# The products that find the softmax maxima read fp16 copies of queries and keys, in the first two softmax attentions

## The chip, the cores and the metric

The kernel runs on one core of one Trainium2 chip. The time is device microseconds of that core. Its engines work side by side and meet at semaphores: PE (TensorE; PEld is its weight load), DVE (VectorE), ACT (ScalarE), POOL (GpSimd), and SP, which issues transfers. Matrix products go to PSUM, of which this kernel's attention uses 8 banks.

## The reference

Eight stages work on an `x` of 16 sequences of 128 tokens, 256 channels each, and each stage adds to it: a correlation attention, a quantised feed-forward, a windowed softmax attention, a feed-forward over soft slots, a full softmax attention, a receptance feed-forward, a rotary softmax attention and a routed feed-forward. The change concerns the windowed and the full one. Both compute, with 16 heads of 16 channels,

```python
Q = (query @ Wq.T + bq).reshape(b, s, N_HEADS, HEAD_DIM).transpose(0, 2, 1, 3)
K = (key @ Wk.T + bk).reshape(b, s, N_HEADS, HEAD_DIM).transpose(0, 2, 1, 3)
scores = jnp.einsum('bhqd,bhkd->bhqk', Q, K) * scale
scores = jnp.where(mask[None, None], scores, jnp.float32(-jnp.inf))   # windowed one only
attn = jax.nn.softmax(scores, axis=-1)
out = jnp.einsum('bhqk,bhkd->bhqd', attn, V)
```

where the query is the layer-normalised `x`, and key and value are the context. A softmax is the same whatever value is subtracted from a row's scores, so the maximum that is subtracted need not be exact.

## The kernel before

`attention` runs three times: windowed, full, and rotary. Its work has two parts.

Projections. PE projects keys, values and then queries; a job is one half of the channels (`o`, 2 of them) of four sequences (`g`, 4 groups). ACT writes the keys to `KT` and the queries, in two variants by the parity of the head, to `QT` (two activations a job, L978); both are fp32. The first maxima are made inside: PE's query jobs go g = 0, 1, 2, then `maxima(0)`, then g = 3. In the windowed and the full attention DVE has nothing to do in the query projections until then.

The loop over tiles. A tile is one sequence, n = 0 to 15, with its 16 heads. For each tile the scores are computed twice. `maxima(n)` on PE (L824) makes them with the queries in the rows: for each of HR = 4 slots and R = 4 groups of 32 partitions, a product with 32 x 128 weights (`QT`) and 128 columns (`KT`). DVE reduces them over the keys, in two instructions of two banks each (L1105), to negated maxima in bf16. PE turns these (L831), ACT copies them out (L989). `scores(n)` (L844) makes the scores again, with the keys in the rows, 8 products of 256 columns, and `shift(n)` (L855) adds the negated maxima with 16 products in bf16, again of 32 x 128 weights and 128 columns. ACT takes the exponentials (L995, two instructions), `weigh_values` (L867) multiplies by the values, ACT copies the sums (L1007), PE turns them (L874), DVE divides (L1111, L1114), PE turns the attended rows (L881), ACT copies (L1002), PE multiplies by the output weights (L888), DVE adds to `X` (L1120). In the windowed attention `add_window` (L807) writes the mask to the banks ahead of maxima and scores.

PE's order in an iteration n is written out by hand: turn_maxima(n), maxima(n+1), turn_sums(n-2), output(n-3), scores(n), turn_attended(n-2), shift(n), weigh_values(n-1). DVE's is maxima(n+1) first half, add_bias(n), normalise(n-2), add_output(n-3), maxima(n+1) second half, statistics. ACT's is attended_out(n-2), exponentials(n) first half, sums_out(n-1), maxima_out(n+1), exponentials(n) second half. `hold_clock` (L55) gives PE products that nobody reads, at the ends and in the first two iterations.

The scores go round a ring of 6 banks, 4 for a tile. So `scores(n)` waits for DVE's first half of `maxima(n+1)`, whose banks it takes over, and for the exponentials of the tile before; `maxima(n+1)` waits for the first exponentials of tile n-1; `turn_attended(n-2)` waits for `add_output(n-3)`; `shift(n)` waits for the copied maxima.

## Time and profile before

| | us |
|---|---|
| runs, median of three | 2104.43 (2100.67 to 2106.3) |
| profiled execution, its own time | 2108.12 |
| profiled execution, span from first to last instruction | 2105.8 |
| PE busy | 1866.5 (89%) |
| DVE busy | 1507.5 (72%) |
| ACT busy | 1122.6 (53%) |

The mean granted clock of TensorE over the span was 0.953 of full speed. The profile is one execution. A row of a timeline gives the start from the span's beginning, the time until the end of the last instruction that is merged into the row, and in brackets how long the engine had been idle and what ended that. An fp32 product leaves two records, so 16 of them are "x32"; a 16-bit one leaves one. In "at_ps<-at_KT,at_QT" the tile written stands left; "32*128" is the part of the array in use. The windowed attention lies at about 327 to 483 us of the span, the full one at 1386 to 1525; the rotary one enters its loop near 1670.

### The profile page before, as it was taken

Reading aid. Unit: us, or ns where it says so; the run is one execution under the profiler, and the core shown is the slowest. Engines: PE = TensorE matmul, PEld = TensorE weight load, DVE = VectorE, ACT = ScalarE, POOL = GpSimd, SP = SyncE. Lnnn points to the kernel's source line nnn. Section 1 sums busy time; section 2 is a strip of 40 time slices with the busy share of each in tenths; the row PEclk is TensorE's granted clock in tenths of the full one; section 3 lists DMA queues with packets and bytes.
Section 4 is the critical chain, followed back from the end, with each engine's and each line's share of the span. In section 5 each row is a group of like instructions: output and inputs, shape, how many; then the busy total and the mean of one; then the engine's idle time right before and its main releaser. Section 6 shows DMA issues by size and latency. Waiting matters only on the chain. (4 is left out here: it accounts for less than half of the span.)

```text
span 2105.8 us, 42222 instructions
## 1 busy us (share of the span) xinstructions
PE 1866.5 (89%) x16876; PEld 1371.4 (65%) x16876; DVE 1507.5 (72%) x3163; ACT 1122.6 (53%) x1896; POOL 155.6 (7%) x121
## 2 busy tenths in 40 slices
PE   7969268997799999999999999989896898599995
PEld 6844055765377766666667777656674577598884
DVE  6887875566777777777777776766666666688886
ACT  3536754446256656666666655435441455366772
POOL 0001300000000000000000000000000000144441
PEclk9979689998999999999999999999999999699997
DMA  6120001002100000000000000010001001567775
GB/s 216 46 77 0 0 1 52 2 3 91 41 21 21 21 21 21 24 33 26 21 21 21 1 1 1 1 51 2 2 21 54 1 2 35 172 226 259 258 239 188
DMA packets 80370, 120.98 MB, mean 57 GB/s; under 512 B 9841, under 2 KB 62513, under 8 KB 80049
## 3 DMA queue, kind: packets, MB, share of 16 engines
q1 hardware_dynamic: 75760, 106.22, 15.2%
q0 software_dynamic: 4416, 12.06, 1.6%
q8 instruction: 136, 2.23, 0.4%
q14 instruction: 58, 0.47, 0.1%
HBM read 103.58 MB, written 14.68 MB: 56 GB/s over the span
## 5 line engine op out<-in xcount | busy, mean ns | idle before, releaser
L2523 PE MATMUL sl_ps_eo<-sl_w,sl_hT 128*128 128x256 f16 x3072 | 354.2, 274 | 0.8 <-DVE sl_hT L2766 0.7
L2500 PE MATMUL sl_ps_h<-sl_slot_inT,sl_w 128*128 128x512 f16 x1536 | 339.1, 380 | 0.5 <-ACT sl_h L2643 0.5
L2523 PEld LDWEIGHTS sl_ps_eo<-sl_w,sl_hT 128*128 128x128 f16 x3072 | 299.1, 98 | 36.3 <-DVE sl_hT L2766 1.3
L2643 ACT ACTIVATE sl_h<-sl_ps_h,sl_b1T 128x512 f32<-128x512 f32 x256 | 175.7, 687 | 171.0 <-PE sl_ps_h L2500 163.9
L2500 PEld LDWEIGHTS sl_ps_h<-sl_slot_inT,sl_w 128*128 128x128 f16 x1536 | 150.2, 98 | 176.7 <-ACT sl_h L2643 2.4
L2766 DVE TENSOR_TENSOR sl_hT<-sl_h,sl_hT 128x512 f16<-128x512 f32 x256 | 176.9, 692 | 102.1 <-ACT sl_hT L2646 97.8
L1105 DVE TENSOR_REDUCE at_neg_max<-at_ps 128x8 bf16<-128x1024 f32 x96 | 116.9, 1221 | 127.4 <-PE at_ps L824 127.4
L2062 PE MATMUL mo_ps_h<-mo_xgT,mo_w 128*128 128x256 f16 x1104 | 126.4, 275 | 2.7 <-issue 1.4
L2780 DVE SCALAR_TENSOR_TENSOR sl_result<-sl_ps_eo,sl_b 128x256 f32<-128x256 f32 x128 | 54.3, 424 | 97.6 <-PE sl_ps_eo L2523 93.2
L2073 PE MATMUL mo_ps_eo<-mo_w,mo_hT 128*128 128x256 f16 x1104 | 124.1, 273 | 0.0
L2062 PEld LDWEIGHTS mo_ps_h<-mo_xgT,mo_w 128*128 128x128 f16 x1104 | 108.4, 99 | 17.9 <-issue 4.3
L2073 PEld LDWEIGHTS mo_ps_eo<-mo_w,mo_hT 128*128 128x128 f16 x1104 | 107.1, 98 | 12.0
L995 ACT ACTIVATE at_probT<-at_ps 128x1024 f32<-128x1024 f32 x96 | 98.6, 1027 | 19.4 <-PE at_ps L855 19.4
L2125 ACT ACTIVATE mo_h<-mo_ps_h,mo_b 128x256 f32<-128x256 f32 x184 | 77.4, 478 | 55.3 <-issue 51.1
L1166 POOL MEMSET at_v<- 128x2048 f32 x6 | 10.7, 1817 | 1140.7 <-POOLq L85 1140.7
L1002 ACT ACTIVATE at_attT<-at_ps 128x256 f32<-128x256 f32 x48 | 18.4, 384 | 140.4 <-PE at_ps L881 140.4
L2145 POOL DMA_INDIRECT mo_xg<-x_rows,mo_from_i x46 | 65.5, 1425 | 237.3 <-DVE mo_from_i L2236 222.0
L2646 ACT ACTIVATE sl_hT<-sl_h 128x512 f16<-128x512 f32 x128 | 80.6, 629 | 4.1
L2622 ACT ACTIVATE sl_combT<-sl_ps_lt 128x512 f32<-128x512 f32 x32 | 19.1, 597 | 110.3 <-PE sl_ps_lt L2479 110.3
L1552 PE MATMUL qf_ps<-qf_xqT,qf_w_inT 128*128 128x512 f16 x288 | 67.0, 394 | 8.6 <-DVE qf_xqT L1751 6.2
L2254 DVE SCALAR_TENSOR_TENSOR mo_w<-mo_w_raw,mo_w 128x1024 f16<-128x1024 f32 x46 | 56.0, 1220 | 15.3 <-ACT mo_w L2107 15.3
L2248 DVE TENSOR_TENSOR mo_hT<-mo_h,mo_hT 128x512 f16<-128x512 f32 x92 | 63.8, 693 | 3.2
(429 smaller groups left out, 3674.4 us busy)
## 6 DMA issues: line engine op xcount, KB each, us to landing
mo_w_raw<-in_L_ffn_W SPq DMA_DIRECT2D x46, 1024.0 KB, 7.7
sl_w_in<-in_L_ffn_w SPq DMA_DIRECT2D x16, 1024.0 KB, 5.3
at_ctxT<-ctx_pairs SPq DMA_DIRECT2D x9, 512.0 KB, 7.6
mo_w_raw<-pair_rows SPq DMA_DIRECT2D x4, 1024.0 KB, 8.9
mo_b<-in_L_ffn_b SPq DMA_DIRECT2D x23, 128.0 KB
ac_attention_w<-L_attention_w SPq DMA_DIRECT2D x3, 768.0 KB, 11.6
w_pairs<-ac_w_pair SPq DMA_DIRECT2D x3, 768.0 KB, 3.2
ac_ctx_all<-in_ctx SPq DMA_DIRECT2D x4, 512.0 KB, 8.2
```

What stands on the lines that cost most here:

```text
L995: act.activation(probT[:, n % 2, 2 * pair:2 * pair + 2].rearrange("p r j q -> p r (j q)"), ps[:, at:at + 2], ACT.Exp, scale=SCALE).then_in ...
L1105: dve.tensor_reduce(neg_max[:, 2 * pair:2 * pair + 2, 0:HR], ps[:, at:at + 2].rearrange("p r (j k) -> p r j k", j=HR), AX.X, ALU.max, nega ...
L1552: last = pe.matmul(pair(q)[:, g], w_inT[:, w, i, k, c * P:(c + 1) * P], xqT[:, x, k, tokens], start=(k, a) == (0, 0), stop=(k, a) == (C - ...
L2062: last = pe.matmul(ps_h[:, q % 3, j % 2], w1_of(m, wp)[:, k, j * P:(j + 1) * P], xgT[:, m % 2, xp, k], start=(k, a) == (0, 0), stop=(k, a) ...
L2073: last = pe.matmul(ps_eo[:, s, 0:D], hT[:, m % 2, hp, j, s * P:(s + 1) * P], w2_of(m, wp)[:, j], start=(j, a) == (0, 0), stop=(j, a) == (H ...
L2125: act.activation(h[:, q % 2, j % 2], ps_h[:, q % 3, j % 2], ACT.Relu, bias=b1[:, m % WB, j:j + 1], scale=1.0 / W_SCALE).then_inc(h_ready, 1)
L2145: pool.indirect_dma_start(xg[:, m % XB, s], None, env.x_rows, bass.IndirectOffsetOnAxis(ap=from_i[:, q:q + 1].bitcast(U32), axis=0)).then_ ...
L2500: last = pe.matmul(ps_h[:, j % 2], w1[:, e % 2, w, k, j * P:(j + 1) * P], slot_inT[:, q % 2, x, k].rearrange("p b s -> p (b s)"), start=(k ...
L2523: last = pe.matmul(ps_eo[:, b % 2, 0:D], hT[:, hp, j, b * P:(b + 1) * P], w2[:, e % 2, w, j], start=(j, a) == (0, 0), stop=(j, a) == (HJ - ...
L2643: act.activation(h[:, j % 2], ps_h[:, j % 2], ACT.Gelu, bias=b1T[:, q // G4, j:j + 1], scale=1.0 / W_SCALE).then_inc(h_ready, 1)
L2646: act.activation(hT[:, 0, j], h[:, j % 2], ACT.Copy).then_inc(h_high, 1)
L2766: dve.tensor_tensor(hT[:, 1, j], h[:, j % 2], hT[:, 0, j], ALU.subtract).then_inc(h_split, 1)
```

## The change

In the windowed and the full attention the operands of L824 are fp16 copies. `QT_half` is a new tile; the keys' copy lies in the memory of the context tile, which is no longer read once all values are projected. DVE makes them: four copies of 1024 elements for the keys and eight of 1024 for the queries in each of the two attentions, placed in its queue ahead of, between and behind the first maxima. PE waits for them ahead of every `maxima(n)`. In the rotary attention the names point to the fp32 tiles, and nothing changes. `scores(n)`, which feeds the exponentials, stays fp32.

```diff
--- before.py
+++ after.py
@@ -651,6 +651,11 @@
         ctxT = t.sb("ctxT", [P, G4 - 1, 2, C, 4, L], F16)
         QT = t.sb("QT", [P, C, B, 2, L])
         KT = t.sb("KT", [P, C, B, L])
+        if rotary:
+            QT_max, KT_max = QT, KT
+        else:
+            QT_max = t.sb("QT_half", [P, C, B, 2, L], F16)
+            KT_max = ctxT[:].rearrange("p g a c b l -> p (g a c b l)")[:, 0:C * B * L].rearrange("p (c b l) -> p c b l", c=C, b=B)
         v1 = t.sb("v1", [P, B, HR, R, 32])
         neg_max = t.sb("neg_max", [P, R, 32], BF16)
         neg_maxT = t.sb("neg_maxT", [P, P], BF16)
@@ -675,6 +680,7 @@
         plain_ready, swap_made = t.sem("plain_ready"), t.sem("swap_made")
         v_made, v_ready = t.sem("v_made"), t.sem("v_ready")
         x_turned, x_high, x_split = t.sem("x_turned"), t.sem("x_high"), t.sem("x_split")
+        k_half, q_half = t.sem("k_half"), t.sem("q_half")
         max_made, max_ready = t.sem("max_made"), t.sem("max_ready")
         max_turned, maxT_ready = t.sem("max_turned"), t.sem("maxT_ready")
         shifted, prob_ready = t.sem("shifted"), t.sem("prob_ready")
@@ -814,6 +820,9 @@
                 if n == 0:
                     pe.wait_ge(proj_out, JOBS + C)
                     pe.wait_ge(v_ready, B)
+                if not rotary:
+                    pe.wait_ge(k_half, G4)
+                    pe.wait_ge(q_half, C * (n // 4 + 1))
                 enough(pe, max_ready, 2 * n)
                 enough(pe, prob_ready, 2 * (n - 2) + 1)
                 if windowed:
@@ -821,7 +830,7 @@
                 for j in range(HR):
                     for r in range(R):
                         rows = slice(32 * r, 32 * r + 32)
-                        last = pe.matmul(ps[:, ring_bank(first, r), j * P:(j + 1) * P], QT[rows, j // 2, n, j % 2], KT[rows, j // 2, n],
+                        last = pe.matmul(ps[:, ring_bank(first, r), j * P:(j + 1) * P], QT_max[rows, j // 2, n, j % 2], KT_max[rows, j // 2, n],
                                          start=not windowed, stop=True, skip_group_check=windowed)
                 last.then_inc(max_made, 1)
 
@@ -1098,6 +1107,15 @@
                 dve.wait_ge(x_high, n + 1)
                 dve.tensor_tensor(xT[:, 1, :, n], x_bank(n), xT[:, 0, :, n], ALU.subtract).then_inc(x_split, 1)
 
+            def keys_half(g):
+                dve.wait_ge(v_made, B)
+                dve.wait_ge(proj_out, C * (g + 1))
+                dve.tensor_copy(KT_max[:, :, 4 * g:4 * g + 4], KT[:, :, 4 * g:4 * g + 4]).then_inc(k_half, 1)
+
+            def queries_half(g, o):
+                dve.wait_ge(proj_out, JOBS + C * g + o + 1)
+                dve.tensor_copy(QT_max[:, o, 4 * g:4 * g + 4], QT[:, o, 4 * g:4 * g + 4]).then_inc(q_half, 1)
+
             def maxima(n, pair):
                 dve.wait_ge(max_made, n + 1)
                 enough(dve, max_turned, n)
@@ -1141,6 +1159,12 @@
                 if rotary:
                     for o in range(C):
                         queries_turned(g, o)
+                else:
+                    if g == 0:
+                        for k in range(G4):
+                            keys_half(k)
+                    for o in range(C):
+                        queries_half(g, o)
                 if g == FIRST_MAXIMA:
                     for pair in range(2):
                         maxima(0, pair)
```

## Rows read from the trace of the kernel before

**Rows 1.** The page, part 1: busy us (share of the span) and instructions by engine.
```profile
PE 1866.5 (89%) x16876; PEld 1371.4 (65%) x16876; DVE 1507.5 (72%) x3163; ACT 1122.6 (53%) x1896; POOL 155.6 (7%) x121
```

**Rows 2.** Table by stretches, full attention: us, busy us by engine, granted clock, DMA.
```profile
1420.00:1520.00 100.00, 92.63 (x1704) 68.55 (x1702) 64.56 (x130) 53.10 (x85) 0.00 (x0) 1.00 0.01 3
```

**Rows 3.** Timeline, a tile of the windowed loop: start, us, engine, line, operation, [idle].
```profile
433.12 0.23 PE L831 MATMUL at_ps<-at_ident_b,at_neg_max 128*128 128x128 bf16 x1
...
433.95 1.17 PE L824 MATMUL at_ps<-at_KT,at_QT 32*128 32x128 f32 x32
...
435.06 0.66 PE L874 MATMUL at_ps<-early_ident,at_sumsT 128*128 128x128 f32 x4
435.19 1.22 DVE L1105 TENSOR_REDUCE at_neg_max<-at_ps 128x8 bf16<-128x1024 f32 x1 [2.81 <-PE at_ps L824]
...
436.53 0.39 PEld L807 LDWEIGHTS at_ps<-at_window_b,at_ident_b 64*64 64x64 bf16 x8 [0.36 <-issue]
...
438.56 0.40 PE L855 MATMUL at_ps<-at_neg_maxT,at_slot_sel 32*128 32x128 bf16 x16
...
438.90 1.08 PE L867 MATMUL at_ps<-at_probT,at_v 128*32 128x128 f32 x32
...
439.91 0.23 PE L831 MATMUL at_ps<-at_ident_b,at_neg_max 128*128 128x128 bf16 x1
```

**Rows 4.** Timeline, a tile of the full attention's loop.
```profile
1492.65 0.23 PE L831 MATMUL at_ps<-at_ident_b,at_neg_max 128*128 128x128 bf16 x1
...
1492.93 1.17 PE L824 MATMUL at_ps<-at_KT,at_QT 32*128 32x128 f32 x32
...
1494.16 1.22 DVE L1105 TENSOR_REDUCE at_neg_max<-at_ps 128x8 bf16<-128x1024 f32 x1 [1.87 <-PE at_ps L824]
...
1495.50 0.77 PEld L844 LDWEIGHTS at_ps<-at_QT,at_KT 32*128 32x128 f32 x16 [0.35 <-issue]
...
1496.26 0.41 DVE L1120 TENSOR_TENSOR X<-X,at_ps 128x256 f32<-128x256 f32 x1
...
1496.78 0.20 PEld L881 LDWEIGHTS at_ps<-early_ident,at_att 128*128 128x128 f32 x2 [0.51 <-DVE at_att L1114]
...
1498.50 0.23 PE L831 MATMUL at_ps<-at_ident_b,at_neg_max 128*128 128x128 bf16 x1
```

**Rows 5.** Timeline, the full attention's last tile, with no L824.
```profile
1510.20 0.23 PE L831 MATMUL at_ps<-at_ident_b,at_neg_max 128*128 128x128 bf16 x1
...
1510.99 0.42 PEld L874 LDWEIGHTS at_ps<-early_ident,at_sumsT 128*128 128x128 f32 x4 [0.69 <-ACT at_sumsT L1007]
...
1511.48 1.03 PE L888 MATMUL at_ps<-at_wo,at_attT 128*128 128x256 f32 x4
...
1512.44 1.15 PE L844 MATMUL at_ps<-at_QT,at_KT 32*128 32x256 f32 x16
```

**Rows 6.** Timeline, full attention, from its query projections into the loop.
```profile
1419.96 2.36 DVE L1105 TENSOR_REDUCE at_neg_max<-at_ps 128x8 bf16<-128x1024 f32 x2 [9.20 <-PE at_ps L824]
1421.33 2.79 ACT L978 ACTIVATE at_QT<-at_ps,at_bq_parity,at_parity_scale 128x512 f32<-128x512 f32 x4 [0.77 <-PE at_ps L755]
...
1424.17 0.23 PE L831 MATMUL at_ps<-at_ident_b,at_neg_max 128*128 128x128 bf16 x1 [0.92 <-ACT at_QT L978]
...
1425.57 1.23 DVE L1105 TENSOR_REDUCE at_neg_max<-at_ps 128x8 bf16<-128x1024 f32 x1 [3.26 <-PE at_ps L824]
```

**Rows 7.** Groups by line and form, DVE, whole span: count, busy us, mean ns.
```profile
L2764 DVE CAST sl_hT<-sl_h 128x512 f16<-128x512 f32 x128 | 53.7, 419 | 3.4 <-ACT sl_h L2643 3.4
...
L2825 DVE CAST sl_row_sel<-early_ident 128x2048 bf16<-128x2048 f32 x1 | 1.2, 1219 | 0.0
```

**Rows 8.** Rotary attention: timeline rows after an idle PE, then a stretch of the table.
```profile
1670.15 0.23 PE L831 MATMUL at_ps<-at_ident_b,at_neg_max 128*128 128x128 bf16 x1 [2.19 <-ACT at_QT L975]
...
1670.31 1.64 PE L824 MATMUL at_ps<-at_KT,at_QT 32*128 32x128 f32 x32
...
1672.50:1675.00 2.50, 2.50 (x23) 2.12 (x26) 2.19 (x3) 0.00 (x0) 0.00 (x0) 0.65 0.00 0
```

## The prediction

> **What bounds the kernel now.** I read the page first, then a table by stretches, then the timeline of one tile in each of the two loops that the change reaches. The page gives TensorE 1866.5 us busy of a span of 2105.8 us [rows 1], but that is an average over eight stages, so it only says where to look. The table for the full attention, from the handover out of its projections to the last tile, shows PE busy 92.63 of 100 us at a granted clock of 1.00, the 2.4 GHz level [rows 2]. A busy PE here is not an engine that nobody holds up. So the question is which wait ends last inside a tile.
>
> The windowed attention repeats a tile every 439.91 - 433.12 = 6.79 us [rows 3], the full one every 1498.50 - 1492.65 = 5.85 us [rows 4]. In both, PE turns the maxima (L831), makes the products for the next maxima (L824), turns the sums (L874), makes the output (L888) and the scores (L844), turns the attended rows (L881), shifts (L855) and weighs the values (L867). What leaves L824 is picked up by DVE at L1105, the first reduction of a pair, and PE may not write the scores until that reduction is done, since they go to its banks. In the full attention the reduction starts at 1494.16, lasts 1.22 and ends at 1495.38; the weights of the scores load at 1495.50, 0.12 later [rows 4]. DVE then goes on with the bias, the reciprocal, the product and the addition at L1120, which ends at 1496.26 + 0.41 = 1496.67, and PE's L881 loads 0.11 later, at 1496.78: this is a real wait, 0.51 long [rows 4]. In the windowed one the same reduction ends at 435.19 + 1.22 = 436.41 and the next PE group loads at 436.53, again 0.12 later [rows 3]. So both tiles are a ring PE L824, DVE L1105, PE scores (in the full one with DVE L1120 behind it), rest of PE. L824 lies in that ring. Whatever it sheds arrives at DVE earlier, and DVE has time: it idled 1.87 us before the reduction in the one and 2.81 in the other [rows 3, 4].
>
> **What the products cost and will cost.** An fp32 product appears as two records, so the 16 products are 32 records of 32*128. They take 1.17 us, and the next group starts 435.06 - 433.95 = 1.11 behind their start [rows 3]. The changed ones are 16 products of 16 bits with the same 32*128 weights and 128 columns. L855 is exactly that shape and count, in bf16: 0.40 us, and the next group starts 438.90 - 438.56 = 0.34 later [rows 3]. I take it for fp16. Gain: 1.17 - 0.40 = 0.77 us for a tile. Bounds: no better than 0.77, since I find nothing shorter of that shape; at worst a product costs what an fp32 record costs now, 1.11 / 32 = 0.035, so 16 take 0.56 and the gain is 0.55.
>
> **The ring with shorter products.** Full attention, counted from L831 at 0 (1492.65). L824 still starts at 0.28 (the exponentials that free its banks hang on L855 and move along); DVE gets the maxima at 0.28 + 0.40 + 0.06 = 0.74 instead of 1.51 (1494.16), ends the first reduction at 1.96 and would let PE go at 2.08. On PE the sums must be turned first, and here a new wait shows: in the last tile, which has no L824, L874 loads at 1510.99, 0.79 behind L831 (1510.20), held by ACT's copy of the sums [rows 5]. PE would otherwise be there at 0.28 + 0.34 = 0.62, so it now waits 0.17. From L874 to the output is 0.49 and from the output to the scores 1512.44 - 1511.48 = 0.96 where nothing stalls [rows 5]. So the scores start at 0.79 + 0.49 + 0.96 = 2.24 instead of 2.88 or so. They last 1.15 [rows 5], and as with L824 (1.17 long, followed after 1.11) the next group can come 0.06 before the modelled end, at 3.33. DVE's own chain to L1120 moves the full 0.77: it released L881 at 4.13 and now does at 3.36. That is the later of the two. The rest of the tile hangs on L881 unchanged. Tile: 5.85 - 0.77 = 5.08 us. The new wait costs nothing because it is hidden under DVE's chain by 0.03 us; if that cover is gone it costs at most its 0.17.
>
> Windowed attention, from L831 at 433.12: products from 0.83, off at 1.17 instead of 1.94. The sums are ready at 0.79, before that. Then 0.49 and 0.96 lead to 2.62; DVE's reduction starts at 2.07 - 0.77 = 1.30, ends at 2.52 and releases at 2.64 instead of 3.41. Tile: 6.02 us, again 0.77 less.
>
> Each layer has 16 such groups, 15 in the loop and one in the projections. For that one: ACT starts the queries' seventh job at 1421.33 after 0.77 idle, so it ended the sixth at 1420.56; it waited because PE made the maxima's products ahead of that job [rows 6]. 0.77 less lets it start at 1420.56: just the full gain. The sum of gains is 2 x 16 x 0.77 = 24.6 us.
>
> **What is added.** 12 copies on DVE in each layer, fp32 to fp16, 1024 elements each: four of keys, eight of queries. Two casts give the price: 512 elements 419 ns, 2048 elements 1219 ns [rows 7], so 419 + 512 x (1219 - 419) / 1536 = 0.69 us, 8.2 us a layer. Bounds: 0.42 (the cast of 512) and 1.22, what DVE takes for 1024 elements one at a time (L1105). I take 0.69, between two casts of the same kind. DVE idled 9.20 us before the first reduction at 1419.96 [rows 6], from 1410.76. Four key copies fill it to 1413.5, and the query copies then follow ACT, which needs 2.79 / 2 = 1.40 for a job [rows 6]. All that PE's first maxima wait for (four key copies, two query copies) is there near 1416, since the second job ends at 1420.56 - 4 x 1.40 = 1414.96, and L824, 1.17 long, begins only some 1.2 ahead of 1419.96. No gain is lost there.
>
> Behind it some is. Copies of the third group stand ahead of the first reduction in DVE's queue: job six ends at 1420.56, its copy at 1421.3, the pair of reductions at 1421.3 + 2.36 = 1423.6. Then come the last two copies, to 1424.25 and 1424.9, and only then the reduction of the second tile. PE, without that, would turn the first maxima at 1424.17 - 0.77 = 1423.4 and hand the second tile's products to DVE at 1425.57 - 1.54 = 1424.03 [rows 6]. It is held to 1424.9: 0.9 us lost, once, in the full attention. Queued behind these copies is all of the loop's DVE work. PE's wait at L831 is shorter than that: the reductions' end at 1423.6 and 0.1 for the signal, 0.3 behind 1423.4, and it is not added. In the windowed attention the window's products put 0.55 more between L831 and L824 (0.83 against 0.28) [rows 3, 4], on both of the maxima in question, so it loses nothing. The two waits that PE gets ahead of each maxima are long met in the loop; they stand where PE already steps over two met waits ahead of L888 without a gap, so I put them at 0, at most 0.03 each (1.8 in all, an estimate from the gap being unseen at the 0.01 us of the rows).
>
> At 1.22 for a copy, DVE would be 5 or 6 us later in all by the same count (about 2.4 in the windowed, 3.5 in the full one).
>
> **Sum.** -24.6 + 0.9 = -23.7 us. Against the profiled execution, 2108.12 us (the span of 2105.8 and 2.3 around it), that is 2084.4. The median of the three runs shown is 2104.43, 3.7 lower, so the forecast of the time is **2080.7 us**.
>
> **Rivals.**
> 1. The products are bound by issue, not by width: a product costs an fp32 record's 0.035 us. Against it stands L855. Gain 32 x 0.55 - 0 = 17.6 (DVE's copies are then covered), time 2086.8.
> 2. The copies run at one element a cycle. For it: nothing shows a cast from fp32 of this very form; against it both casts. Gain 24.6 - 5.9 = 18.7, time 2085.7.
> 3. In the full attention the sums' chain takes over where its cover is 0.03 us thin, and the tile gains 0.17 less: 16 x 0.17 = 2.7, time 2083.4.
> 4. The change does not do what it says: what an fp32 product costs is a fixed price of the instruction, 1.11 / 16 = 0.069 us, and a 16-bit one costs it too. Gain near 0, time 2104. The 16 matmuls of L855, 0.34 / 16 = 0.021 us apart, speak against it [rows 3]. The Trainium skill has a rule of this kind ("TensorE: Matmul & The Clock Gate", the section on the 56 ns gap): with hardware decode off, the sequencer takes about 62 ns for every MATMUL, however short. By that page the products would stay at 16 x 62 = 0.99 us, an estimate, and the change would give 32 x 0.12 = 4 us. The 21 ns between the matmuls of L855 say that it is not in force here.
> 5. Slower than before: the clock. PE does less in each tile. In the third attention, behind an idle PE of 2.19 us, the granted clock of a stretch was 0.65, so for most of it at the 1.2 GHz level, and the same 32 records took 1.64 us instead of 1.17 [rows 8], 1.40 times. The Trainium skill, the same page, in its part on the clock gate, says that the throttled clock is the default and activity lifts it, so less work is a risk in itself; that the dense loops show 1.00 [rows 2] agrees with it. If a tile went that low it would cost 0.40 x 5.1 to 6.0 = 2.0 to 2.4 us. The change turns slower from 11 of the 32 tiles on; with all of them, 32 x 2.2 - 23.7 = +47 us, 2151. Against it: the stretch of rows 2 holds a PE idle of 0.92 us at the handover [rows 6] and last tiles with no L824 at all, and ran at 1.00 throughout. One dip at the handover of the full attention (PE now idles about 1.2 and 0.9 us there) would cost 1 to 2 us and stays in the range.
>
> **Chances.** Forecast 0.72 (2077 to 2084, by the runs' own spread of 2100.67 to 2106.3 and the waits' bounds), rival 1 0.07, rival 2 0.07, rival 3 0.07, rival 4 0.03, rival 5 0.04. The range takes in rivals 1 to 3 and on the low side the runs' spread: 2075 to 2089. A measurement of this kernel can tell about 0.3% (6.3 us) from no change; of the cases only 4 lies within it and only 5 beyond it. So faster 0.93, same 0.03, slower 0.04.
>
> **What would show it.** L824 as 256 records a layer (16 x 16) instead of 512, near 0.40 us a tile; tiles of 6.0 and 5.1 us; a new wait of about 0.2 us of PE at L874 for ACT in the full attention only; 12 DVE casts a layer of 0.69 us, the last two of them between the first pair of L1105 and the second; the second tile's first L1105 in the full attention some 0.7 us earlier than now where 1.54 was to be had. The forecast is wrong if the 16 products take over 0.6, if L881 waits on something other than L1120, or if the granted clock leaves 1.00 inside the loops. The third attention must not move.

## The result, and the profile after

The changed kernel takes 2081.48 us, the median of 4 runs (2073.85 to 2082.91); the kernel before, in 4 runs, 2103.34 (2100.67 to 2106.3). The ratio is 0.9888 with a 95% interval of 0.986 to 0.9916, so 18 to 29 us less. The forecast was 2080.7, in a range of 2075 to 2089. Runs of one kernel spread by 6 to 9 us here, so that forecast and median lie 0.8 us apart is in part luck; the stages below are the sharper measure. The profiled execution took 2081.03 us with a span of 2078.8 and a mean granted clock of 0.955.

The page of the changed kernel, its span and part 1 (answers to [rows 1]):

```profile
span 2078.8 us, 41262 instructions
...
PE 1838.9 (88%) x16364; PEld 1345.4 (65%) x16364; DVE 1522.3 (73%) x3187; ACT 1123.1 (54%) x1896; POOL 152.1 (7%) x121
```

PE has 16876 - 16364 = 512 records fewer, 256 a layer, as 16 products of 16 bits leave 16 records where 16 of fp32 left 32. It is 27.6 us less busy, and DVE, with 24 copies more, 14.8 us more.

The lines have moved: L824 is now L833, L831 is L840, L844 is L853, L855 is L864, L867 is L876, L874 is L883, L881 is L890, L888 is L897, L1105 is L1123, L1120 is L1138, L807 is L813. The copies are at L1113 (keys) and L1117 (queries). First a tile of the windowed loop, from the timeline of the changed kernel (answers to [rows 3]; start, us, engine, line, operation, [idle]):

```profile
416.07 0.23 PE L840 MATMUL at_ps<-at_ident_b,at_neg_max 128*128 128x128 bf16 x1
...
416.90 0.40 PE L833 MATMUL at_ps<-at_ctxT,at_QT_half 32*128 32x128 f16 x16
...
417.24 0.66 PE L883 MATMUL at_ps<-early_ident,at_sumsT 128*128 128x128 f32 x4
417.36 1.23 DVE L1123 TENSOR_REDUCE at_neg_max<-at_ps 128x8 bf16<-128x1024 f32 x1 [2.03 <-PE at_ps L833]
...
418.70 0.39 PEld L813 LDWEIGHTS at_ps<-at_window_b,at_ident_b 64*64 64x64 bf16 x8 [0.34 <-issue]
...
422.07 0.23 PE L840 MATMUL at_ps<-at_ident_b,at_neg_max 128*128 128x128 bf16 x1
```

The products take 0.40 us where they took 1.17, the reduction starts 417.36 - 416.07 = 1.29 behind the turning of the maxima (1.30 forecast, 2.07 before), ends at 418.59, and the window's products load 0.11 later. The tile takes 6.00. Ahead of that load PE's weight loading idles 0.34, where it idled 0.36 before [rows 3]. In the full attention the scores load behind the same output products after 0.33 idle (1421.60 below), though the reduction there has ended 0.29 earlier; so 0.33 is PE's own, and here DVE was late by some 0.03 before and 0.01 now. In the windowed attention PE's own order and DVE's reduction end practically together, and the changed products lie in both.

Then a tile of the full attention's loop (answers to [rows 4]):

```profile
1419.37 0.23 PE L840 MATMUL at_ps<-at_ident_b,at_neg_max 128*128 128x128 bf16 x1
...
1419.64 0.40 PE L833 MATMUL at_ps<-at_ctxT,at_QT_half 32*128 32x128 f16 x16
...
1420.09 1.22 DVE L1123 TENSOR_REDUCE at_neg_max<-at_ps 128x8 bf16<-128x1024 f32 x1 [1.58 <-PE at_ps L833]
1420.15 0.42 PEld L883 LDWEIGHTS at_ps<-early_ident,at_sumsT 128*128 128x128 f32 x4 [0.28 <-ACT at_sumsT L1016]
...
1421.60 1.15 PE L853 MATMUL at_ps<-at_QT,at_KT 32*128 32x256 f32 x16
...
1422.19 0.41 DVE L1138 TENSOR_TENSOR X<-X,at_ps 128x256 f32<-128x256 f32 x1
...
1422.72 0.20 PEld L890 LDWEIGHTS at_ps<-early_ident,at_att 128*128 128x128 f32 x2 [0.37 <-issue]
...
1424.44 0.23 PE L840 MATMUL at_ps<-at_ident_b,at_neg_max 128*128 128x128 bf16 x1
```

The new wait for ACT's sums is there: L883 loads at 1420.15, 0.78 behind L840, after 0.28 idle. The scores start 1421.60 - 1419.37 = 2.23 behind it (2.24 forecast), and L890 loads at 3.35 (3.36 forecast), 0.12 behind the end of DVE's L1138 at 1422.60, as it did 0.11 behind it before. The tile takes 5.07. Over the stretch from 1420 to 1480 the granted clock was 1.00, with 58.20 of 60 us busy.

From the first query product to the last turning of maxima, the windowed attention went from 114.68 us to 101.99 (-12.69; forecast -12.3) and the full one from 99.34 to 87.57 (-11.77; forecast -11.4): -24.5 us together, where -23.7 stood. Of the windowed 12.69, 0.16 is one tile of 6.95 us, the last in the execution before. The other -2.5 of the two spans' 27.0 lie in stages that the change doesn't touch, which vary by that much between executions. The rotary attention is an example: its tile is 5.85 in both, but its stage took 114.16 us before and 112.33 after. The granted clock was 0.51 at its first query products before (1643.5 to 1646) and full after. Of the eight profiled executions whose rotary attention reads fp32, the four with such a stretch there take 26.80 or 26.81 us from the first query product to the first turning of maxima, the four without it 25.12 or 25.13.

The entry of the full attention's loop, from the same timeline (answers to [rows 6]):

```profile
1402.42 0.69 DVE L1117 CAST at_QT_half<-at_QT 128x1024 f16<-128x1024 f32 x1 [0.65 <-ACT at_QT L987]
1403.03 2.35 DVE L1123 TENSOR_REDUCE at_neg_max<-at_ps 128x8 bf16<-128x1024 f32 x2
...
1405.30 1.29 DVE L1117 CAST at_QT_half<-at_QT 128x1024 f16<-128x1024 f32 x2
...
1405.53 0.22 PE L840 MATMUL at_ps<-at_ident_b,at_neg_max 128*128 128x128 bf16 x1 [1.22 <-DVE at_neg_max L1123]
...
1406.50 1.22 DVE L1123 TENSOR_REDUCE at_neg_max<-at_ps 128x8 bf16<-128x1024 f32 x1
```

The last two copies stand between the first pair of reductions and the second tile's, and DVE does not idle between 1402.42 and the end of that third reduction: the queue is the limit here, as forecast. Counted from the first query product, the second tile's first reduction came at 14.71 before and at 13.82 now, 0.89 earlier, of 1.54 that were to be had.

### The profile page after: what moved, and what is told of

Its sections match the earlier page's. It is cut to its first block and busy times, and to the rows that moved or that the text cites. A ratio compares the mean times of both kernels' runs of the same rounds, so it can differ in the third digit from the quotient of the medians.

```text
span 2078.8 us, 41262 instructions
## 1 busy us (share of the span) xinstructions
PE 1838.9 (88%) x16364; PEld 1345.4 (65%) x16364; DVE 1522.3 (73%) x3187; ACT 1123.1 (54%) x1896; POOL 152.1 (7%) x121
## 5 line engine op out<-in xcount | busy, mean ns | idle before, releaser
L1123 DVE TENSOR_REDUCE at_neg_max<-at_ps 128x8 bf16<-128x1024 f32 x96 | 116.9, 1221 | 79.7 <-PE at_ps L833 79.7
L2097 PEld LDWEIGHTS mo_ps_eo<-mo_w,mo_hT 128*128 128x128 f16 x1104 | 107.1, 98 | 12.5 <-issue 0.5
L2278 DVE SCALAR_TENSOR_TENSOR mo_w<-mo_w_raw,mo_w 128x1024 f16<-128x1024 f32 x46 | 56.1, 1221 | 15.5 <-ACT mo_w L2131 12.3
```

The lines of the kernel that those rows point to most:

```text
L1123: dve.tensor_reduce(neg_max[:, 2 * pair:2 * pair + 2, 0:HR], ps[:, at:at + 2].rearrange("p r (j k) -> p r j k", j=HR), AX.X, ALU.max, nega ...
L2097: last = pe.matmul(ps_eo[:, s, 0:D], hT[:, m % 2, hp, j, s * P:(s + 1) * P], w2_of(m, wp)[:, j], start=(j, a) == (0, 0), stop=(j, a) == (H ...
```

## The experiments

The theory to be tested: PE's 16 products lie in the ring through DVE's first reduction in both loops, so their 0.77 us come off every tile; the copies and the waits for them cost nothing but one delay at the full attention's entry. The rivals: the products are bound by something else than their width, the copies cost time elsewhere, the sums' chain takes over.

### The copies and the waits without the shorter products

```diff
-                        last = pe.matmul(..., QT_max[rows, j // 2, n, j % 2], KT_max[rows, j // 2, n],
+                        last = pe.matmul(..., QT[rows, j // 2, n, j % 2], KT[rows, j // 2, n],
```

> All twelve copies and both waits of the change stay, but the products that find the maxima read the fp32 tiles. Theory (ring of the products on PE, the first reduction on DVE, the scores on PE; copies hidden): the products take 1.17 us again, tiles 6.79 and 5.85 us as before, and at the entry of the full attention's loop the last copy ends about 0.7 us ahead of the second tile's first reduction, so nothing is lost: within 1 us of the kernel before. Rival (the copies or the waits cost something on the path): 1 to 6 us slower than before.

Measured: 2100.22 us (10 runs, 2096.33 to 2104.88) against 2102.13 of the kernel before, ratio 0.9993 (0.9979 to 1.0007). Tiles of 6.79 and 5.85 as before; the stages take 114.52 and 99.38 us (114.68 and 99.34 before). A tile of its full attention, from the timeline:

```profile
1471.90 0.23 PE L840 MATMUL at_ps<-at_ident_b,at_neg_max 128*128 128x128 bf16 x1
...
1472.18 1.18 PE L833 MATMUL at_ps<-at_KT,at_QT 32*128 32x128 f32 x32
...
1473.41 1.23 DVE L1123 TENSOR_REDUCE at_neg_max<-at_ps 128x8 bf16<-128x1024 f32 x1 [1.87 <-PE at_ps L833]
```

The products start 0.28 behind L840 as in [rows 4], with two more waits ahead of them: a met wait costs nothing that the rows can show. At the entry, from the timeline of the same kernel:

```profile
1420.24 1.39 DVE L1117 CAST at_QT_half<-at_QT 128x1024 f16<-128x1024 f32 x2
...
1422.36 1.22 DVE L1123 TENSOR_REDUCE at_neg_max<-at_ps 128x8 bf16<-128x1024 f32 x1 [0.73 <-PE at_ps L833]
```

With fp32 products the last two copies end 0.73 ahead of the second tile's reduction and delay nothing. So all of the gain comes from the products, and the entry's loss shows only once they are short.

### The windowed attention alone

```diff
-        if rotary:
+        if not windowed:
             QT_max, KT_max = QT, KT
```

> The change in the windowed attention alone. Theory: its tile 6.0 us, the full attention's stays 5.85, together 16 x 0.77 = 12.3 us faster than before, half and a little more of the change's gain, since the full attention alone loses 0.9 us at the entry of its loop. Rival (the gain of one attention comes mostly from elsewhere, for instance from the clock): a gain far from 12 us.

Measured: 2087.22 us (4 runs, 2083.58 to 2088.97), ratio 0.9935 (0.991 to 0.996), 13.7 us less, with 8 to 19 in the interval. Tiles 6.00 and 5.85; the windowed stage takes 101.99 us and the full one 99.51. The two attentions add up: neither gain depends on the other. (The 0.9 us that the expectation speaks of is measured next.)

### The last copies moved into the loop

```diff
-                    for o in range(C):
-                        queries_half(g, o)
+                    if g < FIRST_MAXIMA:
+                        for o in range(C):
+                            queries_half(g, o)
                 if g == FIRST_MAXIMA:
...
                         maxima(0, pair)
+                    if not rotary:
+                        for o in range(C):
+                            queries_half(g, o)
...
                     maxima(n + 1, 1)
+                if not rotary and n in (4, 5):
+                    queries_half(G4 - 1, n - 4)
```

> The changed kernel with four query copies put later in DVE's queue: those of the third group behind the first pair of reductions, those of the fourth into the fifth and sixth iteration of the loop. Theory: the second tile's first reduction in the full attention no longer waits for copies and comes 0.9 us sooner after the first query job than in the changed kernel, and the copies in the loop fit into DVE's idle 1.09 us of a tile, so the kernel is 0.9 us faster than the changed one, too little for the clock on the wall but not for the timeline. Rival (something else is late next at the entry, the table load or PE): under 0.3 us sooner. Rival (a copy in the loop delays the ring): a tile of 5.07 becomes 5.3 or more where the copies stand.

Measured: 2075.89 us (4 runs, 2074.78 to 2076.66), ratio 0.9876 (0.9852 to 0.9901). The entry, from its timeline:

```profile
1402.72 1.29 DVE L1117 CAST at_QT_half<-at_QT 128x1024 f16<-128x1024 f32 x2
...
1404.68 0.23 PE L840 MATMUL at_ps<-at_ident_b,at_neg_max 128*128 128x128 bf16 x1 [0.92 <-ACT at_QT L987]
...
1405.30 1.23 DVE L1123 TENSOR_REDUCE at_neg_max<-at_ps 128x8 bf16<-128x1024 f32 x1 [1.29 <-PE at_ps L833]
```

PE's turning waits for ACT again, by the 0.92 us of [rows 6], and DVE idles 1.29 ahead of the reduction. That comes 1405.30 - 1392.13 = 13.17 behind the first query product: 1.54 earlier than before, the whole gain. The stage takes 86.92 us instead of 87.57. The place of the entry's loss is shown; its size is 0.65, not 0.9. The tiles that hold a copy stay at 5.07, so DVE has room for one in the loop. In the run times the two kernels can't be told apart.

### Half the columns

```diff
+                half_or_all = P if windowed or rotary else P // 2
...
-... ps[:, ring_bank(first, r), j * P:(j + 1) * P], QT_max[rows, j // 2, n, j % 2], KT_max[rows, j // 2, n],
+... ps[:, ring_bank(first, r), j * P:j * P + half_or_all], QT_max[rows, j // 2, n, j % 2], KT_max[rows, j // 2, n, 0:half_or_all],
```

The reduction (at L1126 in this kernel) reads the same half.

> The changed kernel, but in the full attention the maxima are taken over the first 64 of 128 keys alone: the products have 64 columns and DVE's reductions read half. It leaves out the other half of the keys in the maxima only. Two questions. The 16 products: if their price is the width, the next group comes 0.17 to 0.2 us behind them instead of 0.33; if it is the instruction or the weight load, 0.33 stays. The tile: by my ring for the changed kernel, PE's own order and the wait for ACT's copy of the sums are within 0.03 us of DVE's chain, so halving a reduction (1.22 to about 0.7) saves 0.05 us of 5.07 at most. By the rival that DVE's reduction still sets the tile, it saves 0.4 us or more.

Measured, in one profiled execution: 2074.8 us. A tile of its full attention, from the timeline:

```profile
1440.97 0.23 PE L841 MATMUL at_ps<-at_ident_b,at_neg_max 128*128 128x128 bf16 x1
...
1441.25 0.30 PE L834 MATMUL at_ps<-at_ctxT,at_QT_half 32*128 32x64 f16 x16
...
1441.60 0.69 DVE L1126 TENSOR_REDUCE at_neg_max<-at_ps 128x8 bf16<-128x512 f32 x1 [1.97 <-PE at_ps L834]
1441.75 0.42 PEld L884 LDWEIGHTS at_ps<-early_ident,at_sumsT 128*128 128x128 f32 x4 [0.33 <-ACT at_sumsT L1017]
...
1443.21 1.15 PE L854 MATMUL at_ps<-at_QT,at_KT 32*128 32x256 f32 x16
1443.31 0.42 DVE L1141 TENSOR_TENSOR X<-X,at_ps 128x256 f32<-128x256 f32 x1
...
1444.28 0.20 PEld L891 LDWEIGHTS at_ps<-early_ident,at_att 128*128 128x128 f32 x2 [0.33 <-issue]
```

The durations of single products, min, median and max in ns: the changed kernel, by its line,

```profile
L833 PE MATMUL at_ps<-at_ctxT,at_QT_half x512: 211/214/225, 358.5 to 1475.6; 32*128 32x128 f16 x171
```

and this one's full attention, by its own:

```profile
L834 PE MATMUL at_ps<-at_ctxT,at_QT_half x240: 184/188/198, 1403.6 to 1471.6; 32*128 32x64 f16 x120
```

The group's time less one product, over 15, is the mean step from product to product: (0.40 - 0.214) / 15 = 12.4 ns with 128 columns, (0.30 - 0.188) / 15 = 7.5 ns with 64. The ends are modelled, but the starts of the single records give about the same, 12.7 and 7.3. It is a mean: of four products in the four row groups the starts lie 2 to 5 ns apart, and the next four begin some 55 ns behind the first of them with 128 columns, some 30 with 64. The price falls with the width, so no fixed price of an instruction sets it. (The start of the next group can't be read for this, since L884 now waits for ACT.)

The second reading is the tile: 5.03 to 5.04 us, 0.04 less than 5.07, although DVE has two reductions of 0.69 instead of 1.22 in it. Here DVE's addition (L1141) ends at 1443.73, 0.55 before L891 loads, and what is left is PE's own order behind the sums: L891 idles the 0.33 of "issue", 1.07 behind the start of the scores. This is the cover of 0.03 us that the forecast spoke of. That the sums' chain is the bound at 5.03 is read from the waits (L884 idles 0.33 for ACT's sums); no run makes that chain shorter to test it.

### DVE's chain shorter by the bias, before and after

Both kernels move one DVE addition of 0.42 us behind the one that PE waits for.

```diff
-                if n < B:
-                    add_bias(n)
...
                     add_output(n - 3)
+                if n < B:
+                    add_bias(n)
```

In the kernel before:

> The kernel before, with DVE's addition of the output bias put behind the addition of the output in each iteration. No copies, products in fp32. Theory: in the full attention L881 waits for DVE's chain reduction, bias, reciprocal, product, addition; without the bias (0.33 us start to start) L881 comes at 3.95 us of the tile instead of 4.13, where PE is ready for it, and the tile is 5.68 instead of 5.85: some 2.3 us in all. The windowed attention, bound by PE there, does not move. Rival (PE's own work is the bound and nothing on DVE matters): no change in either.

In the changed kernel:

> The changed kernel with the same reordering on DVE. Theory: with the shorter products the sums' wait and PE's own order stand only 0.03 to 0.04 us behind DVE's chain in the full attention, so the tile gains that and no more: 5.07 to 5.04, about 0.5 us in all, not to be told from the changed kernel by its time. Rival (DVE's chain still holds L881 by its full excess): 2 us or more as in the kernel before.

Measured before: 2100.93 us (10 runs, 2094.64 to 2104.31), ratio 0.9996 (0.9985 to 1.0007). The full tile takes 5.67 us (5.85 before), the windowed one 6.79 as before, and the full stage 97.26 instead of 99.34. The rotary attention has the same DVE order, which the expectation left out of its count, and its tile also takes 5.67; 12 of its tiles were 5.85 before, which makes 2.2 us. So the tiles give some 4.3 us in the two attentions, and the run times do not show them (+1.5 to -3.2 us in the interval). Where that went stays open: no stretch of the profile is longer for it by more than the untouched stages vary.

Measured after: 2073.68 us (4 runs, 2069.95 to 2075.33), ratio 0.9862 (0.9842 to 0.9882). The full tile takes 5.03, the windowed one 6.00, the rotary one 5.67. From the full attention of the changed kernel with that edit, timeline:

```profile
1440.97 0.41 DVE L1138 TENSOR_TENSOR X<-X,at_ps 128x256 f32<-128x256 f32 x1
1441.30 0.42 DVE L1076 TENSOR_TENSOR X<-X,at_bo 128x256 f32<-128x256 f32 x1
...
1441.79 0.20 PEld L890 LDWEIGHTS at_ps<-early_ident,at_att 128*128 128x128 f32 x2 [0.33 <-issue]
```

DVE's addition ends at 1441.38, 0.41 ahead of L890: it is no longer what PE waits for, and L890 idles 0.33, the least that it does in the loops of the kernel before, of the changed one and of this one. Read against that 0.33, the idle time of this one load tells how late DVE is in each kernel: 0.51 before [rows 4], so 0.18, and the edit saved 0.18 us a tile; 0.37 in the changed kernel, so 0.04, and the edit saved 0.04. Two different cuts of DVE's work (this one and the half columns) end at the same 5.03.

### The rotary attention too, with the copies on DVE

The copies of the entry stand as in the kernel with the late copies, and in the rotary attention DVE copies one block in each of nine iterations.

```diff
-        if rotary:
-            QT_max, KT_max = QT, KT
-        else:
+        if True:
...
-                    pe.wait_ge(k_half, G4)
+                    pe.wait_ge(k_half, n // 4 + 1 if rotary else G4)
...
                 if rotary:
+                    if g == 0:
+                        keys_half(0)
                     for o in range(C):
                         queries_turned(g, o)
+                    if g == 1:
+                        for o in range(C):
+                            queries_half(0, o)
...
+                if rotary and n < 12 and n % 4 < 3:
+                    if n % 4 == 0:
+                        keys_half(n // 4 + 1)
+                    else:
+                        queries_half(n // 4 + 1, n % 4 - 1)
```

> The kernel of e3_late_copies with the rotary attention changed too: fp16 copies by DVE, three of them in its projections, nine spread over the loop, one an iteration, behind the second reduction. Theory: its tile is the full attention's, 5.85 to 5.08 us, 12.3 us in all, less about 2 us for three copies of 0.69 in projections where DVE idles in gaps of 0.25 to 1.3 us only: 10 us faster than the changed kernel, about 33 faster than before. Rival (a copy in a tile pushes DVE's ring): tiles with a copy stay above 5.4 us, and the gain is 5 us or less.

Measured: 2064.62 us (4 runs, 2059.71 to 2067.19), ratio 0.9819 (0.9796 to 0.9842), 38 us less than before (33 expected, 33 to 43 in the interval) and some 11 us less than the late copies alone. The rotary tile takes 5.07, with a copy in it or not. From its timeline, a tile with a copy:

```profile
1660.55 0.68 DVE L1111 CAST at_ctxT<-at_KT 128x1024 f16<-128x1024 f32 x1
...
1662.06 1.22 DVE L1121 TENSOR_REDUCE at_neg_max<-at_ps 128x8 bf16<-128x1024 f32 x1 [0.49 <-PE at_ps L831]
```

DVE still idles 0.49 us ahead of the reduction: the copy lies in idle time. The first tile's period was 4.09 where the full attention has 3.37: PE had idled 2.19 us ahead of it, and over that period the granted clock was 0.77, for its last part at the 1.2 GHz level, much as in [rows 8].

### The same copies on GpSimd

```diff
+            if rotary:
+                pool.wait_ge(v_made, B)
+                for g in range(G4):
+                    pool.wait_ge(proj_out, C * (g + 1))
+                    pool.tensor_copy(KT_max[:, :, 4 * g:4 * g + 4], KT[:, :, 4 * g:4 * g + 4]).then_inc(k_half, 1)
+                    for o in range(C):
+                        pool.wait_ge(proj_out, JOBS + C * g + o + 1)
+                        pool.tensor_copy(QT_max[:, o, 4 * g:4 * g + 4], QT[:, o, 4 * g:4 * g + 4]).then_inc(q_half, 1)
```

> As e7_rotary_dve, but POOL makes the rotary attention's copies, which has nothing to do there. No row shows POOL at such a copy. Theory: if one takes under 2 us, those for the first tile are there in time, nothing stands in DVE's queue, and the whole 12.3 us come: 12 to 13 us faster than the changed kernel. Rival: POOL's copy takes several us, the first maxima wait for it, or DVE's instructions get longer while POOL copies; then it is no better than with DVE.

Measured: 2060.76 us (4 runs, 2059.77 to 2065.13), ratio 0.981 (0.9791 to 0.983), which the intervals don't tell from the version on DVE, as the rival said. The tile is 5.07 again, and the first period 3.36. The low clock is not gone, it came earlier, in the projections:

```profile
1630.15 1.60 PE L786 MATMUL at_ps<-at_plain,at_half_swap 128*128 128x512 f32 x2 [1.88 <-ACT at_plain L970]
1631.55 3.60 PE L55 MATMUL at_ps<-early_ident 128*128 128x128 f32 x20
```

PE idled 1.88 us there, the granted clock was 0.58 from 1630 to 1634, and the ten products of L55 took 3.60 us where they take 2.39 in the version on DVE. That is why PE idles only 0.81 ahead of the loop.

From the first query product to the first turning of maxima it takes 26.72 us instead of 24.80 (25.12 in the changed kernel, with no copies). Of these 1.92 us, 1.66 stand already at DVE's first reduction, 18.84 behind the first query product instead of 17.18 and ahead of the low clock; so they are not the clock's. The loop then gives 0.98 back, since the clock is full in it, and the whole stage takes 101.09 us instead of 100.15. The query projections, from the same timeline (L1082 and L1090 are DVE's rotation of the queries):

```profile
1615.74 1.04 POOL L1202 CAST at_QT_half<-at_QT 128x1024 f16<-128x1024 f32 x1 [8.34 <-ACT at_QT L982]
1615.77 1.55 DVE L1090 TENSOR_TENSOR at_q_turned<-at_by_cos,at_by_sin 128x512 f32<-128x512 f32 x1
...
1618.75 1.40 POOL L1202 CAST at_QT_half<-at_QT 128x1024 f16<-128x1024 f32 x1 [1.98 <-ACT at_QT L982]
...
1619.29 1.40 DVE L1082 TENSOR_TENSOR at_by_cos<-at_plain,at_cosT 128x512 f32<-128x512 f32 x1
...
1620.10 1.50 POOL L1199 CAST at_ctxT<-at_KT 128x1024 f16<-128x1024 f32 x1
...
1620.61 0.68 DVE L1082 TENSOR_TENSOR at_by_sin<-at_ps,at_sinT 128x512 f32<-128x512 f32 x1
...
1621.33 0.81 DVE L1090 TENSOR_TENSOR at_q_turned<-at_by_cos,at_by_sin 128x512 f32<-128x512 f32 x1
```

A DVE instruction with both operands in SBUF that meets a running GpSimd copy ends 0.54 us behind the copy's end: 1617.32 against 1616.78, 1620.69 against 1620.15, 1622.14 against 1621.60, and 0.54 or 0.55 in the six other cases of this entry. It takes 0.69 alone, so it does next to nothing until the copy is over. The one whose operand lies in PSUM (by_sin at 1620.61) ran inside a copy and took its usual 0.68. It goes the other way too: the copies that start while such a DVE instruction runs take 1.40 to 1.50 us and end 0.9 behind its end (six of the twelve), the others 1.04. The Trainium skill ("SBUF — State Buffer", Who interferes with whom) has this rule: a DVE instruction with two SBUF inputs contends with a GpSimd one that reads SBUF, one with at most one SBUF input does not, and the issue order decides who blocks. The trace agrees, also in the PSUM case. That the blocked one stands still until the other is done, the page says of DVE's 2-port modes only; the constant 0.54 and 0.9 show it for these instructions.

### All together, and the clock at the rotary entry

The copies on DVE with the bias moved, and then the same with 18 instead of 10 of the products that nobody reads ahead of the rotary loop:

```diff
-            hold_clock(pe, env, ps[:, 0, 0:P], 10 if rotary else 3)
+            hold_clock(pe, env, ps[:, 0, 0:P], 18 if rotary else 3)
```

With 10:

> The kernel of e7_rotary_dve (fp16 products in all three attentions, copies on DVE, placed late) with DVE's bias behind the addition of the output as in e6_bias_late_after. Theory: the tiles of the full and of the rotary attention go from 5.07 to 5.03 us, as measured for the full one in e6, 1.1 us in all; the time is that of e7 less about 1 us, not to be told apart by it. In the loop of the rotary attention the order bias, copy on DVE must not lengthen a tile. Rival (the copy now meets the ring, since the bias stands ahead of the second reduction): tiles with a copy of 5.1 us or more.

With 18:

> As e9_all_three, with 18 instead of 10 of the products that nobody reads ahead of the rotary attention's loop, into the 2.19 us in which PE waits for ACT's queries there. In e7_rotary_dve the scores of the first tile took 1.83 us instead of 1.15 and the stretch's granted clock was 0.65. Theory: eight more products are 1.9 us at the 2.4 GHz level, PE no longer idles over 0.5 us there, the clock stays at 1.00 and the first tile of the loop takes 3.4 us as in e8_rotary_pool instead of 4.1: 0.7 us. Rival (the products run past the queries and delay the turning of the maxima, or the clock falls anyway): no gain, or up to 1 us lost.

Measured: 2061.37 us (4 runs, 2058.51 to 2063.42), ratio 0.9798 (0.9783 to 0.9813), and 2061.1 (5 runs, 2060.09 to 2064.8), 0.9807 (0.9793 to 0.982). Both loops at 5.03, the windowed one at 6.00. PE at the rotary entry, timeline of the version with 10:

```profile
1636.12 0.23 PE L838 MATMUL at_ps<-at_ident_b,at_neg_max 128*128 128x128 bf16 x1 [2.19 <-ACT at_QT L982]
...
1636.82 2.08 PE L55 MATMUL at_ps<-early_ident 128*128 128x128 f32 x8
1638.82 1.56 PE L851 MATMUL at_ps<-at_QT,at_KT 32*128 32x256 f32 x16
```

and of the version with 18:

```profile
1635.53 0.23 PE L838 MATMUL at_ps<-at_ident_b,at_neg_max 128*128 128x128 bf16 x1 [0.41 <-ACT at_QT L982]
...
1636.02 1.16 PE L55 MATMUL at_ps<-early_ident 128*128 128x128 f32 x8
1637.42 1.15 PE L851 MATMUL at_ps<-at_QT,at_KT 32*128 32x256 f32 x16 [0.24 <-DVE at_neg_max L1121]
```

After 2.19 us of idle PE the four products of L55 (eight records) took 2.08 us and the scores 1.56, at a granted clock of 0.61 over that period; after 0.41 they took 1.16 and 1.15, and the granted clock was 1.00, the 2.4 GHz level. The first period was 4.42 and is 3.36. That is 1.06 us once, and the run times don't show it.

That the eight more products keep the clock up is not shown by these two executions. In the kernel with the copies alone PE idled the same 2.19 us, and the table by stretches, from the first turning of maxima on, says:

```profile
1666.00:1670.00 4.00, 3.47 (x65) 2.96 (x69) 2.33 (x3) 1.78 (x3) 0.00 (x0) 1.00 0.02 4
```

There the first period was 4.15, as in the full attention with fp32, where the nine other executions with that idle time have a stretch at the 1.2 GHz level and longer first periods. So the low clock is the usual outcome but not a certain one, and one execution without it may be chance.

Either version is some 2% faster than the kernel before and 1% faster than the change.

## Why the prediction was right, point by point

**Where the products lie.** Right. Both tiles lost what the products lost (6.79 to 6.00, 5.85 to 5.07; 6.02 and 5.08 forecast), and the copies alone gave nothing, so the shorter products are the whole cause. How I found the ring was looser than it looked. I took a gap of 0.11 or 0.12 us between DVE's end and PE's load for proof that PE hangs on DVE, and the idle time of 0.51 for the length of a wait. Of the idle times ahead of these loads, 0.51, 0.36 and 0.35, 0.33 is PE's own each time. At L881 in the full attention 0.18 us were DVE's, which the bias moved in the kernel before confirms; at the scores there and at the window's products the reduction was late by only 0.02 and 0.03. In the windowed attention it was thus as much PE's own order as DVE that set the tile. The forecast is the same either way, since L824 lies in PE's order and in DVE's chain: that the gap did not mislead me there is luck.

**What a product costs.** Right in the sum, 0.40 us for 16. Its reason was read loosely: I took the distance from group to group, 0.34 / 16 = 21 ns, for the step between products. The mean step is 12.4 ns, and the rest is the end of a group. Rival 1 (35 ns for each) and rival 4 (69 ns) fall with the 0.40, and the half columns add that the price falls with the width. By the Trainium skill's 62 ns for a MATMUL ("TensorE: Matmul & The Clock Gate", the section on the 56 ns gap) 16 products could not start in less than 0.93 us, an estimate; all of them were done in 0.40, so its condition, hardware decode off, does not hold in these runs, or the rule not for products in four row groups.

**The new wait.** Right. PE waits for ACT's sums in the full attention (0.78 behind L840; 0.79 forecast) and it costs nothing, by a cover of 0.04 us (0.03 forecast). Rival 3 did not come, but two experiments that shortened DVE's chain ran into it at 5.03.

**The copies.** Their price was right: 694 ns median for one alone, 0.69 forecast, so rival 2 falls. In a row they are cheaper: two take 1.29 us, so the second adds 0.60.

**The entry.** The mechanism was right and the term too large: the loss was 0.65 us, not 0.9. I had the two copies at 0.69 each behind a pair of reductions that ended at 1423.6. In the queue each instruction starts some 0.09 before the modelled end of the one ahead: from the copy at 1402.42 to the pair 0.61, from the pair to the last copies 2.27, from these to the reduction 1.20, together 4.08 where the durations that I added make 0.69 + 2.36 + 1.38 = 4.43. That is 0.35 us, enough for the 0.25 by which the term was too large. The windowed entry lost nothing in PE's order that its stage shows: it gave 12.5 us (114.52 with the copies alone to 101.99), not less than 16 x 0.77 = 12.3.

**The stages gave a little more than 24.6 - 0.9.** Between -23.7 and -24.5 lie 0.8 us. The entry makes 0.25 of them, the one tile of 6.95 in the execution before 0.16, and the tiles, which lost 0.784 and 0.776 where 0.77 stood, some 0.3: 0.7 together.

**The clock.** Rival 5 did not come: 1.00 from the first query product to the last turning of maxima in the windowed and the full attention of all twelve profiled executions, though PE idled 1.22 us at the full one's entry. The rotary entry dips in either kernel, where PE idles 2.19 us. It also varies between executions of the same code, by 1.7 us at the first query products and by about 1 at the loop's start, without the change having a part in it.

## What to carry to other kernels

Find the ring that sets a loop's period, and cut an operation only if it lies in it. A short gap between one engine's end and the next one's load suggests a wait but does not prove it: compare the idle time with the least that the same load shows where nobody holds it up (0.33 us here), and only the rest is the wait. Where that rest is near zero, the engine's own order may set the time just as well, and the operation must lie in both. Then compute at once which chain is next and how much cover is left (here 0.04 us), because that, and not the work removed, bounds a second cut. Products that only find a maximum to subtract need no fp32, and their copies are free on an engine that idles inside the ring, if they are spread one to an iteration and kept out of the stretch between two reductions at the loop's entry. Ask of an idle engine what it shares before giving it the work: GpSimd had nothing to do and with its copies the first maxima still came 1.9 us later than with DVE's own.

## What the runs showed of the hardware

- 16-bit products with 32 rows in four row groups step by 12.4 ns on average with 128 columns and by 7.5 ns with 64; 16 take 0.40 and 0.30 us. The same 16 in fp32 with 128 columns take 1.17 us, 2.9 times as long.
- A DVE copy of 1024 fp32 elements a partition to fp16 takes 0.69 us alone and adds 0.60 behind another. GpSimd takes 1.04 for it, and meanwhile holds up DVE instructions with two SBUF operands until it is done, not those that read PSUM. Such a DVE instruction holds up a copy in the same way, which then takes 1.40 to 1.50.
- PE idle for 2.19 us at the rotary entry goes with a stretch at the 1.2 GHz level, from its end on or within 2.2 us of it, in nine of ten executions, and in one not. Idle for 1.22 or 0.92 us at the other two entries was followed by none in twelve executions. At the rotary attention's first query products, behind 0.98 us of idle PE, four of twelve executions show a low stretch.
